# Unread products of an identity matrix on TensorE in the fusing stage of a gated cross-attention and expert block

## What is computed

```python
x = x + tanh(g_xattn[0]) * attention16heads(layernorm(x), ctx)       # ctx: 8 x 77 x 512
x = x + tanh(g_ffn[0])   * (experts_top2_of_8(n) + two_shared(n))    # n = layernorm(x)
p = softmax(layernorm(x) @ ctx.T)                                    # fusing: 512 x 77 a batch
x = x + tanh(g_xattn[1]) * (p @ ctx)
x = x + tanh(g_ffn[1])   * quantised_conv_ffn(layernorm(x))          # 8-bit tokens, ternary weights
```

## Time and profile before

| what | value |
|---|---|
| median of 3 runs | 1673.55 us (1671.61 to 1675.04) |
| profiled execution | 1673.33 us, span 1671.7 us, mean granted clock 0.935 |
| PE busy over the span | 1510.4 us, 90% |
| DVE busy over the span | 1053.8 us, 63% |
| fusing stage, steps 0 to 7 and its end | from 1124.4 to 1298.7 us of the span |
| DVE busy in 1200 to 1210 us and 1210 to 1220 us | 8.59 and 9.93 us |

### The profile page before, as it was taken

The page is one execution under the profiler, slowest core; times in us unless marked ns, Lnnn a source line. Parts: engine busy times, 40 slices in busy tenths (PEclk is TensorE's granted clock), DMA queues, the critical chain, the costliest instruction groups (busy, mean ns, idle before and its releaser), DMA issues. The chain is left out here.

```text
span 1671.7 us, 24835 instructions
## 1 busy us (share of the span) xinstructions
PE 1510.4 (90%) x8764; PEld 1147.7 (69%) x8764; DVE 1053.8 (63%) x1759; ACT 815.9 (49%) x1448; POOL 743.7 (44%) x666
## 2 busy tenths in 40 slices
PE   6589999999978999989999999988888789999997
PEld 5478788788756888867787788765554455555553
DVE  3468878788728564332332333247996899999995
ACT  2145555555522221213343444325777778888883
POOL 0044344435414675243414100255551878888870
PEclk9789999999978999999999999995766889999998
DMA  3157656666326999735535333459772111111112
GB/s 142 46 182 252 210 207 252 228 212 230 127 85 216 355 356 345 247 120 176 179 105 169 119 107 107 138 145 319 235 258 92 38 39 38 64 63 63 52 51 101
DMA packets 131428, 270.31 MB, mean 162 GB/s; under 512 B 16083, under 2 KB 31443, under 8 KB 129288
## 3 DMA queue, kind: packets, MB, share of 16 engines
q1 hardware_dynamic: 100168, 175.47, 31.2%
q0 software_dynamic: 16624, 62.93, 10.7%
q10 hardware_dynamic: 14544, 30.68, 4.9%
HBM read 145.56 MB, written 122.42 MB: 160 GB/s over the span
## 5 line engine op out<-in xcount | busy, mean ns | idle before, releaser
L243 PE MATMUL e_u_ps<-e_xs,w_shared 128*128 128x512 f32 x720 | 169.4, 396 | 6.4 <-DVE e_sg L1262 6.4
L243 PEld LDWEIGHTS e_u_ps<-e_xs,w_shared 128*128 128x128 f32 x720 | 137.6, 192 | 35.4 <-DVE e_sg L1262 6.5
L2357 PE MATMUL f_banks<-b_xdT,w1h 128*128 128x512 f32 x512 | 146.0, 427 | 14.5 <-POOL b_xdT L2107 9.7
L2133 POOL TENSOR_TENSOR b_h<-b_h,b_srow 128x512 f32<-128x512 f32 x112 | 143.3, 1333 | 26.3 <-ACT b_srow L2169 26.3
L1458 PE MATMUL e_u_ps<-e_w,e_xs 128*128 128x512 f32 x528 | 133.0, 401 | 2.0 <-DVE e_xs L1354 1.2
L2357 PEld LDWEIGHTS f_banks<-b_xdT,w1h 128*128 128x128 f32 x512 | 97.1, 196 | 48.2 <-POOL b_xdT L2107 14.1
L2326 PE MATMUL b_o_ps<-w2q,b_h 128*128 128x512 bf16 x448 | 116.9, 384 | 8.7 <-ACT b_h L2163 8.7
L2158 ACT ACTIVATE b_h<-b_h 128x512 f32<-128x512 f32 x128 | 88.2, 690 | 53.4 <-DVE b_h L2248 52.4
L1362 DVE TENSOR_TENSOR e_hT<-e_r_ps,e_hT 128x256 fp32r<-128x256 f32 x69 | 29.3, 424 | 134.5 <-ACT e_hT L1200 134.5
L1458 PEld LDWEIGHTS e_u_ps<-e_w,e_xs 128*128 128x128 f32 x528 | 95.7, 188 | 23.2 <-DVE e_xs L1354 1.6
L2245 DVE SCALAR_TENSOR_TENSOR b_h<-f_banks,cw,b_h 128x511 f32<-128x511 f32 x128 | 95.2, 744 | 22.1 <-ACT b_h L2152 22.1
(11 more groups left out here) (267 smaller groups left out, 3504.5 us busy)
## 6 DMA issues: line engine op xcount, KB each, us to landing
slots_in_scratch<-e_xs SPq DMA_DIRECT2D x22, 1024.0 KB, 8.3
e_xe<-slots_in_scratch SPq DMA_DIRECT2D x69, 256.0 KB, 2.7
experts_out_scratch<-e_ye ACTq DMA_DIRECT2D x69, 256.0 KB, 2.0
yx_a<-in_w POOLq DMA_DIRECT2D x10, 1024.0 KB, 5.9
xin<-in_x SPq DMA_DIRECT2D x16, 512.0 KB, 5.0
xres<-in_x SPq DMA_DIRECT2D x16, 512.0 KB, 5.3
x_scratch<-x SPq DMA_DIRECT2D x32, 256.0 KB, 3.4
xn_scratch<-xn SPq DMA_DIRECT2D x32, 256.0 KB, 2.0
```

What stands on the lines that cost most here:

```text
L243: mm = pe.matmul(n.u_ps[:, (2 * q + j) % 4], ws[q // n.KH][:, pa, at:at + P], xs[:, pb, k], start=(k == 0 and (pa, pb) == PASSES[0]), stop ...
L2133: pool.tensor_tensor(ht, ht, srow[:], ALU.mult).then_inc(u_done, 1)
L2357: mm = pe.matmul(f_ps[:, v % RING], n.w1h[:, k, (c - NV) * P:(c - NV + 1) * P], xdT[:, part, k], start=(k == 0 and part == 0), stop=(k == ...
```

## The change

At four places of PE's step unread products are added. Each has `ident_h` as stationary operand and `ident_h`, read four times over, as moving operand, so it streams 512 float16 columns, and each writes the whole first bank of `t_ps`. At that point ACT has copied both banks (the scores L1937 waited for the last copy), and the next step's transposes overwrite it before anybody reads it. Nothing waits for these products, they wait for nothing and raise no semaphore; no other engine's stream changes.

There are 9 of them ahead of the wait for the exponentials, 3 ahead of the wait for the copied probabilities, 1 after each of the output tiles j = 0, 1, 2 and 8 after j = 3: 23 a step, 184 in all.

```diff
+            def keep_busy(count):
+
+                for _ in range(count):
+                    pe.matmul(t_ps[:, 0], ident_h[:], ident_h[:].unsqueeze(1).to_broadcast([P, KD, P]), start=True, stop=True)
+
...
                 if outs:
                     out_transposes(s - 2, par, 0)
                     out_transposes(s - 2, par, 1)
+                keep_busy(9)
                 pe.wait_ge(e_done, s * TB + TB)
                 for j in range(TB):
                     mm = pe.transpose(p_ps[0:C, j], pr[:, j], ident[:])
                 mm.then_inc(p_full, 1)
+                keep_busy(3)
                 pe.wait_ge(p_copied, s + 1)
                 for j in range(TB):
                     if not (isinstance(s, int) and s * TB + j < 2):
...
                     pe.matmul(o_ps[:, j % 2], prT[:, j], craw[:, par], start=True, stop=True).then_inc(o_full, 1)
                     if outs and j in (1, 2):
                         out_transposes(s - 2, par, j + 1)
+                    keep_busy(1 if j < TB - 1 else 8)
```

## The result

| | median us | lowest to highest | executions |
|---|---|---|---|
| before | 1672.58 | 1671.59 to 1675.04 | 4 |
| changed | 1690.56 | 1687.36 to 1702.14 | 4 |

The ratio is 1.0115 [1.0082, 1.0147]: 18.0 us slower, outside the predicted range of 1667.5 to 1677.5. The profiled execution took 1693.66 us with a span of 1691.9 us, 20.2 us more than the span before.

What follows compares the result with a forecast made beforehand. DVE's own work was taken to set the step, PE's half clock costing only where DVE waits. Waits removed, 5.1 us, less falls of 0.8 + 1.5 x 1.6 us, gave 1.9 us off 1673.3: 1671.4 (median 1671.5), range 1667.5 to 1677.5.

Steps and rivals of the forecast that it cites:

- A product costs 0.218 us at full and 0.42 at half clock: Each added product on PE: 0.218 us at 2.4 GHz, 0.42 us at 1.2 GHz.
- The 9, 0.4 us in step 7: Ahead of the exponentials: nine take 1.96 us, covered by idle time except for 0.4 us charged in step 7.
- The 3, nothing: Ahead of the copied probabilities: 0.65 us at full clock, hidden under ACT's copy L1774; 0.5 us late at half clock.
- The single ones, hidden: After the first output tiles: 0.22 us each at full clock, hidden behind DVE; at half clock the last tile comes 0.42 us later.
- The 8 fit at full clock: After the last output tile: eight take 1.74 us at full clock, and the next scores still have 0.7 us to spare.
- The clock falls at the idle 1.6 us ahead of tile 2, in step 1 and one or two more: Likeliest case: PE idles 1.6 us there and the clock falls in two or three steps; 1671.4 us, chance 0.44.
- rival 3: The clock falls among output tiles in steps 1 to 6, so the eight become the bound; about 1679 us, chance 0.18.
- the prediction's own sign of being wrong: Stage shows 0.50 at the nine or eight, DVE waits for L1937 in most steps, or products exceed 0.22 us at full clock.
- A fall costs 1.6 us: At the output tiles: a fall makes the next scores late, 1.8 or 1.3 us, taken as 1.6; 0.8 in step 1.
- After step 7's scores 1.95 us gained: Step 7: 0.45 us at its first output tile and 1.5 us from its two waits of 0.76 us.
- Step 0: First step: 0 to 0.3 us gained, or 3.5 us lost if the clock doesn't rise in time; 0 taken.
- case 5: Something the rows don't show, such as code loading for the longer loop or step 0 gaining its full 2.4 us; chance 0.05.

Runs made afterwards that it cites:

- the repeats: The changed kernel (9, 3, 1, 8) compared again four times with the kernel before, each in its own session: ratios 0.9987, 0.9979, 0.9992 and 0.9983.
- e14: Changed kernel with 12 products in place of 3 behind the transposes of the probabilities (9, 12, 1, 8): ratio 0.9990 to the kernel before.
- e1: First repeat of the unaltered changed kernel (9, 3, 1, 8) against the kernel before: 1670.95 us, ratio 0.9987.
- e8: Third repeat of the unaltered changed kernel (9, 3, 1, 8) against the kernel before: 1672.69 us, ratio 0.9992.
- e9: Changed kernel with two products after each of the first output tiles and 4 after the last (9, 3, 2, 4): ratio 0.9957 to the kernel before.
- the first comparison: The recorded measurement of the changed kernel (9, 3, 1, 8) against the kernel before: 1690.56 us against 1672.58, ratio 1.0115.
- e11: Changed kernel with a further 1 MB DRAM-to-DRAM copy by SP in each of steps 0 to 5: ratio 0.9990.
- e16: Changed kernel (9, 3, 1, 8) with 18 more products ahead of the stage, in PE's wait for the first xn: ratio 0.9989.
- e5: Second repeat of the unaltered changed kernel (9, 3, 1, 8) against the kernel before: 1669.24 us, ratio 0.9979.
- e13: Fourth repeat of the unaltered changed kernel (9, 3, 1, 8) against the kernel before: 1669.22 us, ratio 0.9983.
- e3: Only the 3 products ahead of the copied probabilities, without the 9, the single ones and the 8, against the kernel before: ratio 0.9992.

## Why the prediction was right and wrong

**In the repeats it holds.** It gave 1671.5 us against 1673.55, 2.05 us less; the four repeats average 2.3 us less, each against the kernel before of its own session. Point by point:

- *A product costs 0.218 us at full and 0.42 at half clock*: 0.217 in e14; the nine of e1's step 0 take 3.84 us at half clock (1139.56 to 1143.40), 0.43 each. The figure of 131 ns that the prediction set against it, from the Trainium skill's page "TensorE: Matmul & The Clock Gate", section "Back-to-back issue gap", doesn't hold here: the measurement decides.
- *The 9, 0.4 us in step 7*: the first tile's wait is 0.93 us where 1.29 was expected (1.74 less 0.45). *The 3, nothing*: no cost is seen in the repeats; twelve cost 1.6 us at that tile.
- *The single ones, hidden*: so they are at full clock, but on a misread row. The 1.86 us that the prediction sets against them are one tile of DVE, not two (1.4 to 1.5 us where it doesn't wait for POOL); PE's tile with its transposes and product takes 1.3 us in e1, as it said.
- *The 8 fit at full clock*: right. After the stretch at 1.00 in e1, DVE doesn't wait for the scores of step 3.
- *The clock falls at the idle 1.6 us ahead of tile 2, in step 1 and one or two more*: the place and the size are right (1.62 us in e1's step 3), the count too low: step 1 and three others in each of the four repeats. By rival 3 more than three such falls should have made the kernel slower, and the prediction's own sign of being wrong, 0.50 where PE has the eight, is there in these steps.
- *A fall costs 1.6 us*: the waits for scores behind the falls of e1 are 2.22, 0.77 and 0.21 us and, in step 7, 5.10 - 3.42 = 1.68 us (3.42 is the wait in e8, where the clock held in step 6; predicted 3.2): 1.2 us on average. More falls, each cheaper, and DVE's wait of 1.13 us for POOL in step 2 is gone, which the prediction said would stay: the stretch to step 7's scores came to -0.5 us in e1 (148.60 against 149.06) where the terms give 0.8 + 2.4 - 1.71 - 1.45 = 0.0.
- *After step 7's scores 1.95 us gained*: 398.2 us before, 395.5 in e1, 2.7. That the total came out within 0.3 us is thus in part luck: the count of falls and their price were off in opposite senses, and unchanged code ahead of the stage moves by more than the whole gain.
- *Step 0*: 0 in e1 (wait 2.62 us against 2.40), as the lower bound had it. In e9, where the clock came back before step 0's scores were done, step 1's scores came 25.7 us after L1832 in place of 29.9 in e1, and 4.54 us were lost again at the store, which no step of the prediction had seen.

**In the first comparison it is wrong,** and the step that failed is "*The 3*: 0.65 us at full clock, under ACT's copy L1774 (0.6 us and its hand-over): nothing", with the like sentence on ACT's two copies L1747 for the nine. Both took for granted that ACT begins when PE's transposes are done. There it began 2.4 to 4.8 us later in three steps. The few products were used up at once, PE idled 3.65 to 4.85 us, the clock fell, and the single products and the output tiles then paced DVE at 2.56 us a tile. The only room for it was case 5, "something that these rows don't show", with 0.05 and no price. Rival 3 (the eight as the bound) has the sign, but not the mechanism: the waits for scores in the profile after (1.54, 1.98, 0.29, 2.05, 1.03 us) are of the size that it priced, 6.9 us in sum, and e1 has 3.2 of such.

**What stays open is why ACT began late.** Excluded as sufficient causes are products behind the transposes (e14), a further megabyte of transfer a step in the presence of the products (e11), and an early step 0 (e9, e16); repetition alone doesn't bring it back (e1, e5, e8, e13). Code loading, which case 5 names, doesn't explain it either: between 1250 and 1262 us of after, around step 5's late signal, the two instruction queues moved nothing. One coincidence stands in the rows: the last late start of each of the three steps came 1.4 to 1.5 us behind the end of POOL's last gather of that step (L1703, 1184.42, 1210.81 and 1257.41, against 1185.90, 1212.34 and 1258.79). But the first one of step 3 ended while gathers still ran, and in steps 1 and 4 ACT's L1774 began on time while the gathers ran. What the first comparison's profile has and no other: the view of the DMA issues knows no landing time for the gathers of this stage.

```profile
yx_a<-experts_out_scratch,ycol POOLq DMA_INDIRECT x24
```

```profile
yx_a<-experts_out_scratch,ycol POOLq DMA_INDIRECT x24, 5.0
```

The first is of after, the second of e1, where the gathers land in 5.0 us in the median. Such records are missing in the stage of the experts too, between 500 and 700 us, first of after, then of before:

```profile
slots_in_scratch<-x_a,e_scol POOLq DMA_INDIRECT x64
```

```profile
slots_in_scratch<-x_a,e_scol POOLq DMA_INDIRECT x64, 5.9
```

No time was lost by it there: L1832 starts at 1127.61 in after and at 1127.54 in e1. So the missing records mark this profile as a whole and are no sign of a late signal by themselves. The Trainium skill, page "NOTIFIC — the notification-queue block", section "Overflow: three behaviours, one of which stalls the engine", says that a full queue of such records can, by its setting, stall the engine that writes them or drop new records. Each would fit one of the two findings and neither fits both, and no run here shows it. The kernel before ran undisturbed in the same comparison (1671.59 to 1675.04), so the cause touches the changed kernel and belongs to that session or its chip. It wasn't found.

## What to carry to other kernels

When filler products are to hold TensorE's clock, look at the waits that are left, not at the sum of what is filled: here, step 1 aside, waits of 1.5 to 1.6 us ahead of tile 2 were followed by a fall in three steps of every repeat, waits of 1.1 to 1.2 us in one step or none, and one more product at that place together with four fewer at the end was worth some 0.3% (0.9947 and 0.9957 against 0.9979 to 0.9992). Holding the clock is not the gain itself: the nine alone let it fall in every step from 1 to 6 and still reach 0.9984, since DVE sets the step, and with twelve it held and the time stayed the same. Filler after the last useful product is paid twice over when the clock has fallen, so keep it short. Repeat a surprising comparison in another session before explaining it: the 18 us of the first one belonged to none of the four that followed. When a step becomes earlier, look at which transfer its stores will now meet: 5 MB of weights turned a 4.9 us store into one of 17.4, and moving the weights elsewhere made it worse.

## What the runs showed of the hardware that was not expected

- ACT waited 2.41 to 4.82 us for transposes of PE that were over, in one comparison of five, with a releaser that the profile calls "remote" or gives to a transfer that the code doesn't wait for.
- The time of unchanged code ahead of the stage moves: DVE's first work of the stage starts between 1118.7 (e3) and 1128.1 us (e8) in the profiled executions. A gain of 3 us in the stage can't be read from one total; it was read from L1832 to the scores of step 7.
- PE at half clock was 12.40 of 12.40 us busy (after, 1186.60 to 1199.00) and the clock didn't come back in it; it did so at 1199.1, at the end of the eight.
